# Graph network on one core: in every eighth chunk of layer two a second tile of source rows comes from one-hot products

## What is computed

```python
def _rel_layer(h, src, dst, etype, norm, V, comp, loop_w, bias, activation):
    c = comp[etype]
    m = jnp.zeros((src.shape[0], out_dim), h.dtype)
    for b in range(num_bases):          # 8 bases
        xb = h @ V[b]
        m = m + c[:, b, None] * xb[src]
    m = m * norm
    agg = jax.ops.segment_sum(m, dst, num_segments=h.shape[0])
    out = agg + bias + h @ loop_w
    return jax.nn.relu(out) if activation else out

h = jnp.maximum(_layernorm(x), 0.0)
x = x + rel_layer2(rel_layer1(h))       # both with src, dst, edge types and weights
h = jnp.maximum(_layernorm(x), 0.0)
x = x + gcn(h)                          # conv, relu, conv with degree norms
```

## Time and profile before

| what | before |
|---|---|
| time, median of 3 runs | 2038.98 us (2038.0 to 2039.23) |
| the profiled execution | 2035.34 us |
| its span | 2033.6 us |
| PE, busy share of the span | 83% |
| DVE | 69% |
| POOL | 69% |
| ACT | 18% |
| mean granted clock of PE | 0.898 |
| layer one and what precedes it | up to about 998 us |
| layer two, POOL's part of it | 998 to 1881 us |
| graph convolution | from about 1900 us |

### The profile page before, as it was taken

The page is one execution under the profiler, slowest core; times in us unless marked ns, Lnnn a source line. Parts: engine busy times, 40 slices in busy tenths (PEclk is TensorE's granted clock), DMA queues, the critical chain, the costliest instruction groups (busy, mean ns, idle before and its releaser), DMA issues. The chain is left out here.

```text
span 2033.6 us, 40639 instructions
## 1 busy us (share of the span) xinstructions
PE 1691.0 (83%) x12305; PEld 1214.2 (60%) x12306; DVE 1404.2 (69%) x2294; ACT 356.8 (18%) x869; POOL 1403.0 (69%) x1527
## 2 busy tenths in 40 slices
PE   1488888788788888888389988889999899968998
PEld 1366556566566565566366666666676666745564
DVE  7898888888888878886677566566666657511533
ACT  2032222222222222222101111011011101100300
POOL 5777777777777777777477777777777777777000
PEclk8589889889899899898699888899999899978999
DMA  5334343343343333332222222233232332334473
GB/s 149 92 101 113 94 109 98 96 109 97 92 112 94 93 110 94 98 102 71 72 61 62 60 60 59 58 84 100 85 102 68 82 97 77 92 94 127 148 238 118
DMA packets 194039, 196.66 MB, mean 97 GB/s; under 512 B 109132, under 2 KB 157273, under 8 KB 193946
## 3 DMA queue, kind: packets, MB, share of 16 engines
q0 software_dynamic: 45760, 93.81, 16.8%
q1 hardware_dynamic: 140134, 97.59, 16.5%
q10 hardware_dynamic: 8052, 4.04, 0.7%
HBM read 169.75 MB, written 25.57 MB: 96 GB/s over the span
## 5 line engine op out<-in xcount | busy, mean ns | idle before, releaser
L811 POOL DMA_INDIRECT ring<-h_rows,rel_idx x1312 | 1257.7, 959 | 400.5 <-issue 365.4
L986 DVE TENSOR_TENSOR rel_pick<-rel_src_row,dve_bank 128x1664 bf16<-128x1664 int32 (+1 forms) x268 | 486.0, 1814 | 176.9 <-PE rel_ps_p L1215 93.4
L1284 PE MATMUL rel_ps_z<-rel_C,ring 128*128 128x56 f32 x3100 | 417.9, 284 | 166.6 <-DMA ring<-h_rows,rel_idx 83.2
L1284 PEld LDWEIGHTS rel_ps_z<-rel_C,ring 128*128 128x128 f32 x3100 | 399.4, 200 | 219.0 <-issue 209.8
L1382 ACT ACTIVATE rel_ZT<-rel_ps_z 128x304 f32 x292 | 114.2, 426 | 1071.3 <-PE rel_ps_z L1284 1069.7
L1228 PE MATMUL rel_ps_p<-rel_h_parts,rel_pick 128*128 128x384 bf16 x1150 | 266.8, 363 | 0.0
L1372 ACT ACTIVATE rel_A<-rel_ps_a 128x500 f32 x292 | 165.6, 603 | 391.3 <-PE rel_ps_a L1172 206.2
L1215 PE MATMUL rel_ps_p<-rel_h_parts,rel_pick 128*128 128x384 bf16 x1100 | 202.2, 345 | 22.0 <-DVE rel_h_parts L974 22.0
L1215 PE MATMUL carried<-rel_h_parts,rel_pick 128*128 128x384 bf16 x1100 | 190.7, 332 | 2.4 <-DVE rel_pick L986 2.4
L1172 PE MATMUL rel_ps_a<-rel_M,rel_lo 128*128 128x175 bf16 x784 | 156.8, 296 | 38.3 <-DVE rel_M L953 38.1
L1215 PEld LDWEIGHTS rel_ps_p<-rel_h_parts,rel_pick 128*128 128x128 bf16 x1100 | 113.4, 105 | 100.2 <-issue 39.5
(11 more groups left out here) (232 smaller groups left out, 1699.6 us busy)
## 6 DMA issues: line engine op xcount, KB each, us to landing
ring<-h_rows,rel_idx POOLq DMA_INDIRECT x1312
A_slabs<-rel_A SPq DMA_DIRECT2D x25, 800.0 KB
A_slot<-A_slabs SPq DMA_DIRECT2D x25, 800.0 KB, 4.5
rel_types<-edge_types SPq DMA_DIRECT2D x97, 200.0 KB
early_slot<-A_slabs SPq DMA_DIRECT2D x18, 896.0 KB, 6.1
rel_src_row<-in_src_dram SPq DMA_DIRECT2D x134, 64.0 KB, 3.0
last_slot<-A_slabs SPq DMA_DIRECT2D x4, 512.0 KB, 6.0
ring<-h_rows,idx_table POOLq DMA_INDIRECT x118
```

The costliest lines, as they stand in the source:

```text
L811: g_.indirect_dma_start(ring[:, s * CHUNK + i, :], None, rows_in, bass.IndirectOffsetOnAxis(ap=idx[which][:, n:n + 1], axis=0)).then_inc(l ...
L986: v.tensor_tensor(pick[:, b0:b0 + n, :], src_row[s][:, :].unsqueeze(1).to_broadcast(shape), node_ids[:, b0:b0 + n].unsqueeze(2).to_broadca ...
L1284: ins = m_.matmul(bank(ps_z[s], NB)[:, :, bass.ds(at[i], TW)], ring[:, first + i, :], C[s][:, i, :, :], start=False, stop=(i == n - 1))
```

## The change

In the chunks of ring slot 7 (7, 15, ... 87, eleven in all) layer two now picks two tiles: the last one as before, and the one ahead of it, which POOL no longer gathers. The new tile's source numbers have a buffer of their own, `extra_row`, with its own semaphore, loaded by SP five chunks ahead (`load_extra`). DVE makes its one-hot halves in `make_extra` and adds the parts with `keep_picked`; PE runs `pick_rows` a second time, into the other bank, right behind the first. As there are now nine picks in eight chunks, the counts that the engines wait for are worked out from a new function `place`, and `landings` counts 6 gathers for slot 7.

```diff
--- before.py
+++ after.py
@@ -70,6 +70,7 @@
 PICK_HALVES = ((0, 13), (13, 12))
 PICK_SIXTHS = (((0, 5), (5, 9), (9, 13)), ((13, 17), (17, 21), (21, 25)))
 PICKED = 22 * CPG
+EXTRA = SLOTS_RING - 1
 SOURCES = 4
 SPLIT_GROUPS = 5
 FIRST_PICK, END_PICK = CPG + 1, CHUNKS - 2
...
@@ -733,7 +738,15 @@
         def makes(g, j):
             return layer == 0 and not (isinstance(g, int) and g * CPG + j + AHEAD >= ET_CHUNKS)
 
-        loop = [0]
+        loop = [0, 0]
+
+        def place(parity, j, ahead=0):
+
+            e = parity * CPG + j + ahead
+            return loop[1] * (SLOTS_RING + 1) + (e // SLOTS_RING * (SLOTS_RING + 1) + e % SLOTS_RING)
+
+        def is_picked(c):
+            return layer == 1 and not (isinstance(c, int) and c >= PICKED)
 
         def unit_of(g, j):
 
...
@@ -763,12 +776,18 @@
 
         def gathers(s, late=False):
 
+            if layer == 1 and s == EXTRA and not late:
+                return CHUNK - 2
             return CHUNK if late else CHUNK - (1 if layer == 1 else s % 2)
 
-        def landings(half, s, late=False):
-
-            if layer == 1 and late:
-                return PICKED // 2 * (gathers(s) * 16) + (half - PICKED // 2) * (CHUNK * 16)
+        def landings(half, s, late=False, ahead=0):
+
+            if layer == 1:
+                begun = (s // 2 + ahead) % (SLOTS_RING // 2)
+                odd = s % 2
+                if late:
+                    return PICKED // 2 * (CHUNK * 14 - 4 * odd) + (half - PICKED // 2) * (CHUNK * 16)
+                return half * (CHUNK * 14 - 4 * odd) + 4 * odd * begun
             if layer == 0 and s % 2 == 1:
                 return half * (CHUNK * 16) if isinstance(half, int) and half < 3 else half * (gathers(s) * 16) + 2 * 16
             return half * (gathers(s) * 16)
...
@@ -881,12 +901,19 @@
         else:
             @block.sync
             def _(sp):
-                def load_sources(k, s):
-
-                    after(sp, pick_ready, 2 * (k - (SOURCES - 1)))
+                def load_sources(c, s, freed):
+
+                    after(sp, pick_ready, freed)
                     rows = io["src"].rearrange("(a n) -> a n", a=1)
-                    sp.dma_start(src_row[s][:, :], rows[:, bass.ds(k * (CHUNK * P) + (CHUNK - 1) * P, P)].to_broadcast([P, P]))\
+                    sp.dma_start(src_row[s][:, :], rows[:, bass.ds(c * (CHUNK * P) + (CHUNK - 1) * P, P)].to_broadcast([P, P]))\
                       .then_inc(src_in[s], 16)
+
+                def load_extra(c, freed):
+
+                    after(sp, pick_ready, freed)
+                    rows = io["src"].rearrange("(a n) -> a n", a=1)
+                    sp.dma_start(extra_row[:, :], rows[:, bass.ds(c * (CHUNK * P) + (CHUNK - 2) * P, P)].to_broadcast([P, P]))\
+                      .then_inc(extra_in, 16)
 
                 def load_early(u, s):
 
...
@@ -975,16 +1005,26 @@
 
             split_chains = Chain(dve, split_chain)
 
-            def make_pick(c, s, turn, halves=(0, 1)):
+            def make_pick(k, s, turn, halves=(0, 1)):
 
                 for h in halves:
                     b0, n = PICK_HALVES[h]
                     if h == 0:
                         dve.wait_ge(src_in[s], (turn + 1) * 16)
-                    after(dve, picked, 2 * c + (h - 1))
+                    after(dve, picked, 2 * k + (h - 1))
                     shape = [P, n, P]
                     v.tensor_tensor(pick[:, b0:b0 + n, :], src_row[s][:, :].unsqueeze(1).to_broadcast(shape),
                                     node_ids[:, b0:b0 + n].unsqueeze(2).to_broadcast(shape), ALU.is_equal).then_inc(pick_ready, 1)
+
+            def make_extra(k, turn, h):
+
+                b0, n = PICK_HALVES[h]
+                if h == 0:
+                    dve.wait_ge(extra_in, (turn + 1) * 16)
+                dve.wait_ge(picked, 2 * k + (h - 1))
+                shape = [P, n, P]
+                v.tensor_tensor(pick[:, b0:b0 + n, :], extra_row[:, :].unsqueeze(1).to_broadcast(shape),
+                                node_ids[:, b0:b0 + n].unsqueeze(2).to_broadcast(shape), ALU.is_equal).then_inc(pick_ready, 1)
 
             def keep_picked(c, s, slot):
 
...
@@ -1064,12 +1104,19 @@
                     if layer == 1 and j == 3 and not is_first:
                         fin.dve_norm(dve, g - 1)
                     picks_on = layer == 1 and not (isinstance(c, int) and c + 2 >= PICKED)
+                    extra_here = parity == 1 and j == 2 and is_picked(c + 1)
+                    if extra_here:
+                        make_extra(place(parity, j, 1) + 1, loop[1], 0)
+                        keep_picked(place(parity, j, 1), 1 - s, EXTRA * CHUNK + CHUNK - 1)
+                        make_extra(place(parity, j, 1) + 1, loop[1], 1)
                     if picks_on:
-                        make_pick(c + 2, (j + 2) % SOURCES, g + (j + 2) // SOURCES, (0,))
-                    if layer == 1 and not (isinstance(c, int) and c + 1 >= PICKED):
-                        keep_picked(c + 1, 1 - s, (parity * CPG + j + 1) % SLOTS_RING * CHUNK + CHUNK - 1)
+                        make_pick(place(parity, j, 2), (j + 2) % SOURCES, g + (j + 2) // SOURCES, (0,))
+                    if extra_here:
+                        keep_picked(place(parity, j, 1) + 1, s, EXTRA * CHUNK + CHUNK - 2)
+                    elif is_picked(c + 1):
+                        keep_picked(place(parity, j, 1), 1 - s, (parity * CPG + j + 1) % SLOTS_RING * CHUNK + CHUNK - 1)
                     if picks_on:
-                        make_pick(c + 2, (j + 2) % SOURCES, g + (j + 2) // SOURCES, (1,))
+                        make_pick(place(parity, j, 2), (j + 2) % SOURCES, g + (j + 2) // SOURCES, (1,))
                     if layer == 1 and not (isinstance(c, int) and c + 1 >= CHUNKS):
                         match_nodes(c + 1, 1 - s)
                         weigh(c + 1, 1 - s)
...
@@ -1206,11 +1258,11 @@
                         pe.wait_ge(fin.h_new, g)
                 fin.pe_turn(pe, g)
 
-            def pick_rows(c, s):
-
-                after(pe, row_ready, c - 1)
+            def pick_rows(k, s, kept):
+
+                after(pe, row_ready, kept)
                 for h, (b0, n) in enumerate(PICK_HALVES):
-                    pe.wait_ge(pick_ready, 2 * c + (h + 1))
+                    pe.wait_ge(pick_ready, 2 * k + (h + 1))
                     for b in range(b0, b0 + n):
                         ins = m_.matmul(ps_p[s][:, 0:3 * P], pick[:, b, :], h_parts[:, b, :, :].rearrange("p c n -> p (c n)"),
                                         start=(b == 0), stop=(b == SRC_BLOCKS - 1))
...
@@ -1263,8 +1316,11 @@
                         pick_sixth(nth, j, 1)
                     if layer == 0 and not (isinstance(c, int) and c == CHUNKS - 1):
                         load_words(regs[1 - j % 2], c + 1)
-                    if layer == 1 and not (isinstance(c, int) and c + 1 >= PICKED):
-                        pick_rows(c + 1, 1 - j % 2)
+                    if is_picked(c + 1):
+                        k, e = place(parity, j, 1), (parity * CPG + j + 1) % SLOTS_RING
+                        pick_rows(k, 1 - j % 2, k if e == 0 else (0 if isinstance(c, int) and c < 1 else k - (2 if e == 1 else 1)))
+                        if e == EXTRA:
+                            pick_rows(k + 1, j % 2, k)
                     if layer == 1:
                         load_words(regs[0], c)
                         at = positions(regs[0])
...
@@ -1275,8 +1331,10 @@
                     s, n = sum_edges(g, c, j, at)
                     first = (parity * CPG + j) * CHUNK
                     for i in range(n):
-                        if layer == 1 and i == CHUNK - 1 and not (isinstance(c, int) and c >= PICKED):
-                            pe.wait_ge(row_ready, c + 1)
+                        if is_picked(c) and parity * CPG + j == EXTRA and i == CHUNK - 2:
+                            pe.wait_ge(row_ready, place(parity, j) + 2)
+                        if is_picked(c) and i == CHUNK - 1:
+                            pe.wait_ge(row_ready, place(parity, j) + 1)
                         if picks_here and i == HALF:
                             pick_sixth(nth, j, 2)
                         if layer == 0 and i == CHUNK - 1 and j % 2 == 1 and not (isinstance(c, int) and not first_picks(c)):
```

28 lines of the change are left out of this document (20 added, 8 removed).

## The result

| | before | after | difference |
|---|---|---|---|
| median of 4 timed runs | 2038.49 us | 2017.12 us | -21.4 us |
| timed again on another chip (13 and 4 runs) | 2036.65 us | 2013.68 us | -23.0 us |
| the profiled execution | 2035.34 us | 2014.24 us | -21.1 us |
| its span | 2033.6 us | 2012.5 us | -21.1 us |

The ratio after to before is 0.9890 (95% interval 0.9879 to 0.9902), timed again 0.9888 (0.9871 to 0.9904). One thing is needed to read the experiments: on four of the chips that they ran on, the kernel before itself took 2533 to 2564 us, so that times from there are compared with those of the kernel before beside them only, and one of the ten runs of pick_fourth, at 2424.67 us, counts in no ratio.

The account below looks back on a forecast made before the run. POOL was taken to bound layer two, with PE waiting for it. The profiled 2035.34 us less 13.75 for 11 gathers, all else nil, gave 2021.6, or 2025.2 us for timed runs; range 2018.5 to 2032.5.

Parts of the forecast that it names:

- The bound: Layer two: POOL has no slack from first to last gather, PE waits for it, 76.7 us in 41 waits.
- One gather less in every eighth chunk: POOL, layer two: 11 gathers go, each priced at its pitch of 1.25 us, saving 13.75 us.
- The estimate of 2.15 us per gather: POOL: alternative price for a 64 KB gather, 23.7 us for 11; set aside for the traced pitch of 1.25.
- The second pick on PE: PE, layer two: 25 more matmuls each time, 4.5 us at full clock including 0.4 us of signals; 49.5 us for 11.
- PE keeps up: PE, layer two: 63.2 us fit into 76.7 us of waits; it lags POOL by 11.3 us mid-layer, recovering by chunk 95.
- 14 us of waits: Sign in the profile after: PE's waits for landings near 14 us at the same clock, more if it improves.
- Rival 1: End of layer two: PE's clock recovers too, saving another 4.3 us, giving 2020.9 us; chance 13%.
- Rivals 2 and 3: PE's second picks over 5.7 us lose part of the gain (2031.6, 9%); from 7.0, PE's lag stops POOL (2055.8, 5%).
- Rivals 4 and 5: POOL's gathers slow beside DVE's comparisons, 12.8 us, no change (3%); the end stays since later work has its own times (3%).
- DVE and the loads: DVE's extra 4.2 us eleven times and SP's 11 more loads of source numbers: cost nil.

Follow-up runs that it names:

- pick_fourth: Changed kernel, but POOL still gathers all seven tiles, the superfluous one into a tile nobody reads; 2037.72 us, ratio 1.0002 to the kernel before.
- less_pad1: Kernel before with 55 gathers per eight chunks, no second pick, and one semaphore increment more per eight chunks in POOL's program; 2011.66 us.
- before_pad1: Kernel before with one semaphore increment more per eight chunks in POOL's program, gathers unchanged at 56; 2035.19 us.
- shift3: Kernel before with three more gathers, into a tile nobody reads, ahead of layer two's first; 2545.68 us beside 2535.56 of the kernel before.
- pick_third: Changed kernel, but POOL still gathers all seven tiles, one into a tile nobody reads; 2598.6 us beside 2564.22 of the kernel before, ratio 1.0148.

## Why the prediction was wrong

**The bound: right.** POOL sets the end before and after. PE still waits at chunk 95, and the last gather, not PE's added work, moved the end: pick_fourth gives PE and DVE the second pick and leaves POOL's gathers, and nothing moves (1.0002); less_pad1 takes POOL's gathers away without a second pick, and the time falls by 23.5 us, in single runs.

**"One gather less in every eighth chunk", 11 x 1.25 = 13.75 us: the step that failed.** The mechanism was right and this term was too small: 22.1 us came off POOL's stream and not 13.75. The term is right for the gathers and leaves out the stalls that go with them, 8.84 us. POOL's stretch from gather 25 to the last took 847.47 us before and 824.94 after: 22.5 us. That 0.30 us stand "before every gather" and the next follows 1.25 us after it "through the whole layer" was false at six places. The evidence stood in the earlier trace rows: 180.2 us in 574 waits, the longest 2.0. 574 x 0.30 is 172, so 8 us were not steps of 0.30. The prediction read the sum and the count and passed over the third number. Even so, nothing in the trace of before told that the stalls would go; but the range was built as if all 10.1 us of them were sure to stay, and the case that they shrink belonged in it. The estimate of 2.15 us per gather, worked out from the Trainium skill ("DMA: Bandwidth & Descriptors", on the anatomy of a software-generated DMA), would have given 23.7 us, near the measured 22.1 by accident: the gathers that are left still take 1.25 us each.

**The second pick on PE: 4.5 us, of which the 0.4 us for DVE were too much** (1.0 us of waits in all, not 4.4; and in the earlier trace rows DVE's comparison ended 0.04 us behind PE's pick, which ended at 1650.77, not 0.2). Its cover held, as pick_fourth shows.

**"PE keeps up": right in course, off in size.** PE's lag stood through chunks 43 to 87, with two waits left there where there had been 16, and POOL was never held (its waits for PE are 0.3 us each). What was left of the lag at chunk 88 was about 4 us and not 11.3: PE's waits from there to chunk 91 were 16.1 us before and 12.0 after. Expected were 14 us of waits "if the clock is as before, more if it improves"; 41.8 were left. Eleven picks of 4.2 us and 21 us less time would have taken 67 of the 76.7 us; 34.9 went. So PE's other work took some 32 us less (a rough figure: in before_pad1, with the same work as before, the waits come to 84.0 us and not 76.7, which makes it 25). The clock rose with it. What stood from 1400 to 1790 and from 1790 to 1855 before stands 21 us earlier now:

```profile
1379.00:1769.00 390.00, 385.59 (x2651) 272.40 (x2651) 275.83 (x407) 42.69 (x136) 297.53 (x329) 0.99 0.32 88
1769.00:1834.00 65.00, 50.47 (x299) 37.47 (x297) 14.13 (x44) 6.54 (x20) 49.19 (x54) 0.82 0.38 113
```

The clock (the third number from the end) was 0.96 and 0.76 there before and is 0.99 and 0.82 now. The first rise is in pick_fourth too (0.98 from 1400 to 1790); the second is not (0.76 from 1790 to 1855) and may be chance. **Rival 1** had this mechanism, but it looked for the gain at the end, and there it did not come: chunk 95's edges still ran 3.65 us, at half clock, after a wait of 5.25. Only the early unit behind them was shorter, 5.67 us for 7.21, and before_pad1, without a second pick, has 5.64 there, so that is not the change's doing. The clock's gain went into PE's waits instead. The Trainium skill ("TensorE: Matmul & The Clock Gate", on oscillation) has it that waits for DMA between bursts of matmuls throttle the array again. The traces agree in the middle of the layer: in pick_fourth, with waits for rows of 12.2 us and not 23.2 between 1380 and 1790, the clock is 0.98 and not 0.96. The end did not move by it.

**Rivals 2 and 3** did not happen on the chips that the forecast was for. On the three others where the second pick was run alone, their mechanism did: PE late, POOL waiting for it, and 39, 45 and 34 us more (1.3 to 1.8%), most of the whole 11 x 4.2 = 46.

**Rivals 4 and 5** fell: the gathers average 945 ns as before, and the end moved with POOL. **DVE and the loads: nil, as forecast.**

**The landing.** Some 1.3 us were given back at chunk 95, where PE starts later after the last gather. This was in no step. With it the profile closes: 2035.34 - 13.75 - 8.84 + 1.3 = 2014.05, measured 2014.24.

**What the stalls are stays open.** Shown: they come with 56 gathers in a round and not with 55, stand at one place of the program every second round, do not depend on the second pick, on an instruction more or less, or on three gathers more before the layer's loop. What POOL waits for there is not shown. An obvious candidate, that the next part of the program is being loaded, finds no support in the trace: from 1250 to 1340 us of the kernel before, around the stall at 1286.7, it has packets of the two data queues only and none of the instruction queues. 54 or 57 gathers per round weren't tried, nor was POOL's program shortened by more than one instruction.

## What to carry to other kernels

When a rate is read off an engine's steady rhythm, multiply it back: count times rhythm against the stretch, and look at the longest wait beside the mean. What is left over (here 8 us of 180) may go or come with the change, and belongs in the range. Take the two halves of a trade apart on the chip (less work here, more work there): here one half was the whole gain (single runs), and the other nothing within 2.4 us (ten runs). And work that is free because an engine waits is free only where it waits: on other chips the same second pick cost 34 to 45 us of its full 46.

## What the runs showed of the hardware that was not expected

- POOL's stream of gathers stood still for 1.6 to 1.7 us more than usual every 112 gathers (142.1 us) with nothing in the program to wait for, at the same six places of the program in every profile with 56 gathers a round (there up to 2.3 us, and 3.9 once, on the chips where the kernel before takes 2034 to 2041 us); with 55 a round, 0.4 to 0.7 us were left at one or two places on these chips.
- Between chips, the same kernel took 2034 to 2041 us on some and 2525 to 2573 us on four others, with a mean granted clock of 0.90 and of 0.79 to 0.80. On the four all engines wait for "issue" far more often (PE 277 us in 350 waits in shift3, 3.9 us in 14 in the kernel before on a usual chip), and all but PE for "remote" too. POOL waits for PE there, 105 us in pick_third, which it does not on the usual chips. Why these chips differ is not shown.
- PE did its other work some 15 to 22 us faster when a second pick filled a part of its waits (pick_fourth against before_pad1 and before), with no effect on the time beyond 2.4 us.
